# A three-layer graph network on one core: early loads into idle buffers, gamma and beta applied in SBUF, E turned in the freed PSUM bank, new orders on every engine

## The reference, cut to what matters

```python
h = jnp.maximum(_layernorm(x, axis=-1), 0.0)
x_ = h
for l in range(3):
    scores = si[:, :, None] + sj[:, None, :] + attn_b[l]   # si, sj = x_ @ attn_w[l, :d], x_ @ attn_w[l, d:]
    scores = jnp.where(scores >= 0, scores, 0.2 * scores)
    attn = jax.nn.softmax(jnp.where(mask, scores, -jnp.inf), axis=-1)
    h = layernorm(x_ + attn @ x_, g1[l], beta1[l])
    ff = gelu(h @ W1[l] + b1[l]) @ W2[l] + b2[l]            # 256 -> 1024 -> 256
    x_ = layernorm(h + ff, g2[l], beta2[l])
out = x + x_
```

## Time and profile before

| | us |
|---|---|
| median of 3 runs | 1242.56 (1242.36 to 1243.44) |
| the profiled execution | 1241.6 |
| its span | 1239.8 |
| busy: PE, DVE, ACT, POOL | 1196.4, 1075.9, 920.0, 677.4 |

### The profile page before, as it was taken

One profiled execution on the slowest core, in us unless ns is written; L12 is line 12 of the kernel. 1 busy time (PEld: TensorE's weight loads), 2 busy tenths in 40 slices (PEclk: granted clock), 3 DMA queues, 4 the chain that ended last, 5 costly groups with the idle time before them and its releaser, 6 DMA issues.

```text
span 1239.8 us, 23072 instructions
## 1 busy us (share of the span) xinstructions
PE 1196.4 (97%) x7509; PEld 1082.8 (87%) x7509; DVE 1075.9 (87%) x3568; ACT 920.0 (74%) x1754; POOL 677.4 (55%) x648
## 2 busy tenths in 40 slices
PE   2699999999999999999999999999999999999997
PEld 1589999998999999999999999999999999999996
DVE  5899889999998888899998888899989988888865
ACT  3786887678877776778778767777887777677752
POOL 1354455456755554456666545554666455545564
PEclk9999999999999999999999999999999999999999
DMA  7122322233332111222432122122432321122221
GB/s 256 38 77 73 99 70 60 77 94 112 103 103 88 50 44 52 85 71 85 129 114 92 43 59 70 44 69 78 125 115 80 100 60 43 44 69 61 78 89 48
DMA packets 109620, 100.57 MB, mean 81 GB/s; under 512 B 12952, under 2 KB 95932, under 8 KB 109500
## 3 DMA queue, kind: packets, MB, share of 16 engines
q1 hardware_dynamic: 109500, 99.10, 26.3%
HBM read 66.47 MB, written 32.60 MB: 80 GB/s over the span
## 4 chain that ended last, share of the span: by engine, by line
PE 95%; DVE 3%; SPq 1%; DMA 1%; issue 0%; POOL 0%; ACT 0%; DVEq 0%; POOLq 0%
PE acc L1073 44%; PE hbank L1058 42%; PE mix L1087 7%; PE mix L1112 2%; DMA adji<-in_adj_dram 1%; DVE xs L757 0%; DVE junk L694 0%; DVE st L603 0%; DVE st L764 0%; SPq L313 0%; PE util L1104 0%; SPq L332 0%; DVE sc L729 0%; POOL rstd L467 0%; DVE hid_lo L615 0%
## 5 line engine op out<-in xcount | busy, mean ns | idle before, releaser
L1073 PE MATMUL acc<-w2hi,hid_hi 128*128 128x256 f32 x1536 | 442.2, 288 | 0.0
L1073 PE MATMUL acc<-w2hi,hid_lo 128*128 128x256 f32 x1536 | 434.5, 283 | 0.0
L1073 PE MATMUL acc<-w2lo,hid_hi 128*128 128x256 f32 x1536 | 434.4, 283 | 0.0
L912 ACT ACTIVATE hbank<-hbank,vec 128x512 f32<-128x512 f32 x384 | 255.4, 665 | 178.1 <-PE hbank L1058 167.0
L1058 PE MATMUL hbank<-ht_hi,w1hi 128*128 128x512 f32 x768 | 305.7, 398 | 3.6 <-DVE hid_lo L615 2.0
L1058 PE MATMUL hbank<-ht_lo,w1hi 128*128 128x512 f32 x768 | 300.7, 392 | 0.0
L1073 PEld LDWEIGHTS acc<-w2lo,hid_hi 128*128 128x128 f32 x1536 | 294.0, 191 | 6.9
L1073 PEld LDWEIGHTS acc<-w2hi,hid_hi 128*128 128x128 f32 x1536 | 293.9, 191 | 6.9
L1058 PE MATMUL hbank<-ht_hi,w1lo 128*128 128x512 f32 x768 | 299.3, 390 | 0.0
L615 DVE TENSOR_TENSOR hid_lo<-hbank,hid_hi 128x512 fp32r<-128x512 f32 x384 | 259.9, 677 | 39.4 <-ACT hid_hi L918 39.4
L1073 PEld LDWEIGHTS acc<-w2hi,hid_lo 128*128 128x128 f32 x1536 | 293.9, 191 | 0.0
(11 more groups left out here) (80 smaller groups left out, 1708.4 us busy)
## 6 DMA issues: line engine op xcount, KB each, us to landing
z_dram<-tz SPq DMA_DIRECT2D x46, 512.0 KB, 2.6
zt<-z_dram SPq DMA_DIRECT2D x184, 128.0 KB, 2.8
sj_bc<-sj_dram SPq DMA_DIRECT2D x47, 256.0 KB, 3.9
xraw<-in_x_dram SPq DMA_DIRECT2D x16, 512.0 KB, 4.1
out_dram<-xout SPq DMA_DIRECT2D x32, 256.0 KB, 3.0
xres<-in_x_dram SPq DMA_DIRECT2D x15, 512.0 KB, 5.0
xout<-in_L_gnn_W_dram SPq DMA_DIRECT2D x10, 512.0 KB, 5.5
adji<-in_adj_dram SPq DMA_DIRECT2D x16, 256.0 KB, 3.5
```

The lines of the kernel that those rows point to most:

```text
L912: act.activation(hbank[k % HB][:], hbank[k % HB][:], ACT.Gelu, bias=b1c(i.l, c)).then_inc(gelu_n, 1)
L1073: mm = pe.matmul(to, v[:, k % HID, of_g], w[:, i.l, c], start=c == 0 and n == 0 and g % HG == 0, stop=c == C - 1 and n == 2, skip_group_ch ...
```

## The change: what it does, and the diff

- Item 2's x is loaded early into zt; the adjacencies of items 1 and 2 go into the two halves of tz (EARLY = 2). The head's loads are issued in another order.
- From item 2 on ACT applies gamma and beta on the turned rows in place in zt; the cast and the subtraction then read zt, and write ht_hi and ht_lo in blocks. The move of the next z waits for `h_low` in place of `h_out`.
- E is turned in the bank util, which this frees, in place of mix[0]. PE waits before each write of util for all of its readers.
- All lists have another order, the heads' and the slots'. An "o" is item s-2.

```diff
--- before.py
+++ after.py
@@ -43,7 +43,7 @@
 HID = 4
 HB = 3
 PENS = 4
-EARLY = 1
+EARLY = 2
 LEAD = 3
 BY_PE = 2
 QD = 32
@@ -115,7 +115,9 @@
         diag = sb("diag", [P, P], BF16)
         attn_bias = sb("attn_bias", [P, L])
         vec = sb("vec", [P, NV])
-        fence = sb("fence", [P, 1])
+        spare = sb("spare", [P, 1 + L])
+        fence = spare[:, 0:1]
+        attn_part = spare[:, 1:1 + L]
         dots = sb("dots", [P, 3, GG])
         negm = sb("negm", [P, GG])
         den = sb("den", [P, GG])
@@ -131,7 +133,8 @@
 
         vec_rows = sc[0:NV, 0, 0:P]
         b2_rows = hb[:, 1, 0:L]
-        early = [hb[:, i] for i in range(EARLY)]
+        early = [hb[:, 0], zt[:].rearrange("p m a g t -> p (m a g t)").rearrange("p (g d) -> p g d", g=GG)]
+        early_adj = tz[:].bitcast(I32).rearrange("p c g t -> p (c g t)").rearrange("p (i g j) -> p i g j", i=EARLY, g=GG)
 
         def b1c(l, c): return vec[:, l * C + c:l * C + c + 1]
         def dcol(n, l, m):
@@ -158,6 +161,7 @@
         w_in = [sem(f"w_in{i}") for i in range(4)]
         adj_in = sem("adj_in")
         early_in = [sem(f"early_in{i}") for i in range(EARLY)]
+        early_adj_in = [sem(f"early_adj_in{i}") for i in range(EARLY)]
         xraw_in = sem("xraw_in")
         xres_in = sem("xres_in")
         out_sent = [sem(f"out_sent{i}") for i in range(2)]
@@ -232,6 +236,14 @@
                 return early[i.q - 1], early_in[i.q - 1], 16
             return xraw, xraw_in, 16 * (i.g + 1 if i.q == 0 else i.g + 1 - EARLY)
 
+        def by_block(t):
+            return t.rearrange("p (g a t) -> p a g t", g=GG, a=NQ)
+
+        def adj_of(i):
+            if 1 <= i.q <= EARLY:
+                return early_adj[:, i.q - 1], early_adj_in[i.q - 1], 16
+            return adji[:], adj_in, 16 * (i.g + 1 if i.q == 0 else i.g + 1 - EARLY)
+
         def si_of(i):
             return dots[:, 2 * (i.q % 2)]
 
@@ -320,8 +332,10 @@
                 sp.dma_start(t[:], group(x, i.g)).then_inc(arrived, 16)
 
             def load_adj(i):
-                wait(sp, edge_n, i.g)
-                sp.dma_start(adji[:], group(adj, i.g)).then_inc(adj_in, 16)
+                t, arrived, _ = adj_of(i)
+                if arrived is adj_in:
+                    wait(sp, edge_n, 1 if i.q == 1 + EARLY else i.g)
+                sp.dma_start(t, group(adj, i.g)).then_inc(arrived, 16)
 
             def load_weights(n):
                 if n >= len(halves):
@@ -357,7 +371,9 @@
                 if i.q < BY_PE:
                     return
                 sp.wait_ge(z_sent, 16 * moved(i.q))
-                sp.wait_ge(ht_n, KD * i.q)
+                if i.q == BY_PE:
+                    sp.wait_ge(x0_n, GG * (i.q + 1))
+                sp.wait_ge(htlo_n, KD * i.q)
                 for b in range(NQ):
                     sp.dma_start(zt[b * QD:(b + 1) * QD].rearrange("p m a g t -> p m a (g t)"),
                                  z_dram.rearrange("(a p) (m b f) -> b p m a f", a=NQ, b=NQ, m=KD)[b]).then_inc(zt_in, 16)
...
@@ -479,8 +493,8 @@
                 gs = slice(h * HG, (h + 1) * HG)
                 if i.q == 0 and h == 0:
                     pool.wait_ge(ln1_ready, 1)
-                if i.q < EARLY and h == 0:
-                    pool.wait_ge(x0_n, GG * (i.q + 2))
+                if i.q == 0 and h == 0:
+                    pool.wait_ge(x0_n, GG * 2)
                 pool.wait_ge(z1_n, GG * (i.q + 1) if h else GG * i.q + HG)
                 if i.q >= 2:
                     pool.wait_ge(y2_n, 2 * (i.q - 2) + h + 1)
...
@@ -709,8 +727,9 @@
 
                 if i.q == 0:
                     dve.wait_ge(const_set, 5)
-                dve.wait_ge(adj_in, 16 * (i.g + 1))
-                dve.scalar_tensor_tensor(out=pen[:, i.g % PENS], in0=adji[:], scalar=2 * BIG,
+                edges, arrived, count = adj_of(i)
+                dve.wait_ge(arrived, count)
+                dve.scalar_tensor_tensor(out=pen[:, i.g % PENS], in0=edges, scalar=2 * BIG,
                                          in1=diag[:].unsqueeze(1).to_broadcast([P, GG, P]),
                                          op0=ALU.mult, op1=ALU.add).then_inc(edge_n, 1)
                 dve.wait_ge(edge_n, i.g + 1)
...
@@ -773,127 +792,131 @@
 
             def h_low(i, m):
                 dve.wait_ge(hthi_n, KD * i.q + m + 1)
-                dve.tensor_tensor(ht_lo[:, i.q % 2, m], util[:], ht_hi[:, i.q % 2, m].bitcast(F32),
-                                  ALU.subtract).then_inc(htlo_n, 1)
+                if i.q < BY_PE:
+                    dve.tensor_tensor(ht_lo[:, i.q % 2, m], util[:], ht_hi[:, i.q % 2, m].bitcast(F32),
+                                      ALU.subtract).then_inc(htlo_n, 1)
+                else:
+                    dve.tensor_tensor(by_block(ht_lo[:, i.q % 2, m]), zt[:, m],
...
@@ -930,15 +953,17 @@
                                    scale=g1c(i.l, m)).then_inc(ht_n, 1)
                 else:
                     act.wait_ge(zt_in, MOVES_Z * moved(i.q))
-                    act.wait_ge(htlo_n, KD * i.q + m)
-                    act.activation(util[:].rearrange("p (g a t) -> p a g t", g=GG, a=NQ), zt[:, m], ACT.Identity,
+                    act.activation(zt[:, m], zt[:, m], ACT.Identity,
                                    bias=beta1c(i.l, m), scale=g1c(i.l, m)).then_inc(ht_n, 1)
 
             def h_high(i, m):
                 h_out(i, m)
                 act.wait_ge(ht_n, KD * i.q + m + 1)
                 wait(act, ffn1_n, C * (i.q - 1))
-                act.copy(ht_hi[:, i.q % 2, m], util[:]).then_inc(hthi_n, 1)
+                if i.q < BY_PE:
+                    act.copy(ht_hi[:, i.q % 2, m], util[:]).then_inc(hthi_n, 1)
+                else:
+                    act.copy(by_block(ht_hi[:, i.q % 2, m]), zt[:, m]).then_inc(hthi_n, 1)
 
             def leaky(i):
                 act.wait_ge(mask_n, i.q + 1)
@@ -956,9 +981,9 @@
                                    accum_out=den[:, g:g + 1]).then_inc(exp_n, 1)
 
             def et_out(i):
+                wait(act, agg_n, 2 * i.q)
                 act.wait_ge(et_n, i.q + 1)
-                wait(act, agg_n, 2 * i.q)
-                act.copy(ET[:], mix[0][:].rearrange("p g (e i) -> p (g e) i", i=P)).then_inc(eto_n, 1)
+                act.copy(ET[:], util[:].rearrange("p (g i) -> p g i", g=GG)).then_inc(eto_n, 1)
 
             def first_x(i):
                 act.wait_ge(nmr0_n, i.g + 1)
...
@@ -382,26 +398,26 @@
                 sp.dma_start(xraw[:], group(x, NG - 1)).then_inc(last_in, 16)
 
             def slot(s):
-                t, a, d, q6 = item(s - 1), item(s + 2), item(s + 3), item(s + 6)
+                o, t, b, a, d, p, q6 = item(s - 2), item(s - 1), item(s + 1), item(s + 2), item(s + 3), item(s + 4), item(s + 6)
+                if b:
+                    move_z(b)
+                if q6 and q6.l == 0:
+                    load_adj(q6)
+                load_weights(s + 5)
                 if d:
                     send_sj(d)
                 if t and t.l == L - 1:
                     load_xres(t)
+                if p and p.l == 0:
+                    load_xraw(p)
+                if o and o.l == L - 1:
+                    send_out(o, 1)
                 if d:
                     load_sj(d)
-                load_weights(s + 6)
                 if a:
                     send_z(a)
-                if q6 and q6.l == 0:
-                    load_adj(q6)
-                if a:
-                    move_z(a)
                 if t and t.l == L - 1:
                     send_out(t, 0)
-                if q6 and q6.l == 0:
-                    load_xraw(q6)
-                if t and t.l == L - 1:
-                    send_out(t, 1)
                 if s == ITEMS - 4:
                     load_last_input()
 
...
@@ -1088,37 +1112,46 @@
                                    start=g % HG == 0, stop=True, skip_group_check=True)
                 mm.then_inc(agg_n, 1)
 
+            read = {"e": 0, "z": 0, "s": 0}
+
+            def wait_util_read():
+                wait(pe, eto_n, read["e"])
+                wait(pe, htlo_n, read["z"])
+                wait(pe, mask_n, read["s"])
+
             def sj_rows(i):
                 pe.wait_ge(dotj_n, i.q + 1)
                 pe.wait_ge(vec_ready, 1)
+                wait_util_read()
+                read["s"] += 1
                 for g in range(GG):
                     mm = pe.transpose(util[:, g * P:(g + 1) * P], dots[:, 1, g:g + 1].to_broadcast([P, P]), ident[:])
                 mm.then_inc(sj_n, 1)
 
             def z1_turn(i, m):
-                wait(pe, htlo_n, KD * i.q + m)
-                if i.q == 0 and m == 0:
-                    pe.wait_ge(mask_n, 1)
+                wait_util_read()
+                read["z"] += 1
                 for g in range(GG):
                     pe.wait_ge(z1_n, GG * i.q + g + 1)
                     mm = pe.transpose(util[:, g * P:(g + 1) * P], x_of(i)[:, g, m * P:(m + 1) * P], ident[:])
                 mm.then_inc(zt_n, 1)
 
```

(17 more changed lines are left out.)

240 lines of the change are left out of this document (121 added, 119 removed).

## The result

The changed kernel takes 1285.51 us (median of 4 runs, 1281.32 to 1286.02) beside 1242.46 (1241.97 to 1243.44) for the one before, run with it: ratio 1.0338, 95% interval 1.0326 to 1.0351. The forecast was 1238.4, in a range of 1233.0 to 1243.5; it was wrong in sign. None of the rivals was the cause either.

What follows compares the result with a forecast made beforehand. PE was taken as the bound, busy 1196.4 of 1239.8 us. Head -4.3, late ET slots -2.2 and ffn1 cuts +2.3 gave -4.2: 1237.4 profiled, 1238.4 as a median, range 1233 to 1243.5.

Steps and rivals of the forecast that it cites:

- Part 1, the head: First 60 us: earlier loads and new orders let slot 1 begin earlier, taken at -4.3 us, between 0 and 6.5.
- The lower clock: Head: PE may come back at half speed after standing still some 4 us before 48; 0 to 2 us, taken as 0.
- The 1.00: Granted clock shown by the profile windows, set against item 0's slow aggregation (3.78 us, 1.73 later) being a low clock.
- slot 1 begins 4.3 us earlier: End of the head: slot 1 was to begin near 74.5 us in place of 78.85.
- Part 2, E in util: Slots: turning E in util keeps transposes and copy size, and its three new waits are on work long done; 0 us.
- Part 3, in place: Gamma and beta in zt: 0 to 0.1 us for ACT's pair; DVE's low part 0.6 us as before.
- Part 4, the slot of a steady item: ET in time by 0.1 us, late slots gone (-2.2), six ffn1 blocks (+2.3), period near 24.7 us.
- Part 4, SP and DVE in the slots with a new group: DVE's list adds up to 24.9 us, a mask waiting for sj takes 0.6 more, and both hide.
- each us past 1.37: Slots: ffn2 needs the residuals 1.37 us into the slot; without cover, lateness costs PE only the time beyond that.
- (b): Rival, slots: ET is a little late in each, 0.08 us over 45 slots, +3.6, 1242.0 us; chance 0.14.
- (c): Rival, head: it gives little, through lower clock (2 us) and slips in DVE's list (1 or so); 1241.4 us, chance 0.12.
- (d): Rival, slots: z reaches zt late, so its read-out delays ET's copy; 0.26 a slot, 11.7 us, 1250; chance 0.10.

Runs made afterwards that it cites:

- e5_in_place_alone: The kernel before, with its own orders and loads, plus gamma and beta in place in zt and E turned in util: 1257.14 us, ratio 1.0119.
- experiments 1 and 6: 1: sj's load issued earlier in the changed kernel (1284.15, 1285.27 us); 6: work moved to another place in e9_first_no_place (1253.07, 1271.24, 1304.8 us).
- e1_slot: The changed kernel, with SP issuing sj's load right behind sj's own store in every slot: 1284.15 us, ratio 1.034.
- e12_spread: e9_first_no_place with load, moments and shift of a new group at their slots of the kernel before: 1304.8 us, ratio 1.0494.
- e2_both: e1_slot, and in the head item 3's sj load also goes ahead of the late row loads: 1285.27 us, ratio 1.0344.
- experiment 2: The run e8_store_first, which changes SP's order of transfers in the slots: 1258.40 us, ratio 1.0131.
- e15_pen_early: e9_first_no_place with a new group's adjacency load and penalty one slot earlier: 1253.07 us, ratio 1.0086.
- e9_first_no_place: e8_store_first with the in-place part undone (gamma and beta through util again, E turned in mix[0]): 1261.55 us, ratio 1.0152.
- e8_store_first: e2_both, but in the slots SP issues the output's second-half store and xres ahead of sj both ways, then xraw: 1258.40 us, ratio 1.0131.
- e16_pool_old: e9_first_no_place with POOL's h_beta at its place in the kernel before: 1271.24 us, ratio 1.0233.

## Why the prediction was wrong, point by point

- **Part 1, the head.** Right as far as the placing went: item 0's turn of E 20.07 and aggregation 22.29, norm and turn 34.69 (33.6 forecast), the first turn of item 1 at 49.19 (48.05). The lower clock, 0 to 2 and taken at 0, took about 1.5: behind a stop of 2.94 us matmuls of 256 columns come 0.12 apart and then 0.21, and the granted clock of after falls to 0.50:

```profile
50.95 0.38 PE L1097 MATMUL acc<-w2hi,hid_hi 128*128 128x256 f32 x1
51.14 0.42 PE L1097 MATMUL acc<-w2lo,hid_hi 128*128 128x256 f32 x1
...
51.00:54.40 3.40, 3.40 (x13) 2.92 (x13) 3.36 (x17) 2.06 (x6) 2.48 (x3) 0.50 0.00 0
```

  The 1.00 that the prediction set against a low clock in the head was a reading of 10 to 20 us, ahead of the slow aggregation at 27.30, and the trace of before has no granted clock up to 43.7 us. `e5_in_place_alone`, whose head has the same orders, reads 0.50 from 35 to 44 us, where item 1's aggregation is as slow as item 0's.

  What failed was the step "slot 1 begins 4.3 us earlier". It began 1.7 earlier: 1.1 went in DVE's list and 1.5 in the clock. In slot 1 PE then stood 3.39 us for item 3's sj, sent at 70.4, whose way back is issued behind three late row loads (1.3 MB) and takes 6.76 us. That list had been placed up to 52 us and not beyond.
- **Part 2, E in util.** 0, and right: behind the head no wait of PE before util shows.
- **Part 3, in place.** ACT right (0.04, inside the bounds of 0 and 0.1). DVE wrong: "nearest row the split of twice the size, so 0.6 as now". The split of that row ran with POOL idle. Against POOL's multiplications the same form took 1.35, and cost 14.6 us in the old orders. In the new ones it cost nothing more (0.68 to 0.69), which was luck and not the argument.
- **Part 4, the slot of a steady item.** Right: 24.70 forecast as "near 24.7", 24.70 measured; ET in time there, with aggregations of 1.73, six blocks of ffn1 at +0.05.
- **Part 4, SP and DVE in the slots with a new group.** This is the step that failed: "a mask waiting for sj behind x and xres would take 0.6 more ... Both hide; what they cost without that cover is each us past 1.37". Three things were wrong in it. The wait was 3.26 and more: 1.3 MB ahead of sj, of which the store was not counted. What the residual waits for was read for DVE and PE alone; it also needs a store to have ended. And DVE's 24.9 us were summed from undisturbed rows of steady slots; with moments, shift, penalty and what POOL holds up it is 27 to 28, which bounds the slot by itself. The rule ("each us past 1.37") counted only the standing still: behind most stops the granted clock fell to 0.50, another 1.7 us each time, a cost that the prediction had for the head alone. The sizes were wrong throughout: 0.6 stood for waits that made these slots up to 5.4 us too long.
- **Rivals.** (b) and (c) did not come: ET was in time. (d) had the right sign with a chance of 0.10 and the wrong transfer: ACT waited for zt nowhere in the steady slots, and 3.0 us in all between 75 and 1260. z's lateness showed in experiments 1 and 6 (15.3 us in `e1_slot`, 10.4 in `e12_spread`) and in slot 2 of `e2_both`. No rival had a price for DVE as the bound, although the page gave DVE 87% and the prediction itself had DVE's list end 0.3 us into the next slot.

What of the 43 us has a run behind it: 27 go with SP's order (experiment 2), and 8.5 with a penalty in the same slot as moments and shift (`e15_pen_early` against `e9_first_no_place`, which itself stands 3.2 above `e8_store_first`). What is left, 10.6, is 9.6 in the spans of the profiled executions (1249.4 and 1239.8). By its periods 2.6 lie in slot 2, 8.0 in the clusters, 6.2 of them in their first slots, where penalty and moments still meet, and 2.2 in the +0.05 of all 44 slots; the 2.2 of the late slots before and some 1.1 us of the head go against them, which makes 9.5. Whether another order of POOL's list would win the clusters' 8.0 back stays open: `e16_pool_old` shows that it matters, by 10 us in the wrong direction, and no better one was tried.

## What to carry to other kernels

Add an engine's list up in the slot that has most to do, not in a steady one, and take DVE's durations from rows where POOL runs beside them: the same instruction had 0.29 and 1.4 us here. In front of a transfer that an engine waits for in order, count every byte that its queue issues first, stores too, and read all that the buffer behind it waits for. When one wait in the head is taken away, ask what the next load in the same queue is before the gain is counted: 6.0 us became 2.4.

## What the runs showed of the hardware

- DVE's smallest instructions are held as long as its large ones: a scalar_tensor_tensor on 4 elements a partition took 0.16 us alone and 1.13 beside POOL, and the mask 0.38 or 1.4. A tensor_scalar with one SBUF operand (`norm2`) is held as well: 400 ns alone, 658 in the long slots; in the mean of the first two layers 653 in after against 428 before, in the last layer 554 against 429. Beside POOL's power of 128x4 (1.07 us) a low part with two SBUF operands was not held (0.69, `e5_in_place_alone`); the port rule cited above, as it is worded, would have it wait.
- A load of 256 KB from DRAM to all partitions took 7.51 us from issue to landing behind 1.3 MB, and a 256 KB store 8.1 behind sj's transfers and two loads of 512 KB (in `e1_slot`).
- Stopping for 3 us can cost PE more than the 3 us: its next 36 matmuls took 6.0 in place of 4.31, at a granted clock of 0.50 for 3.4 us of them. Yet in the head, where DVE set the next wait, keeping its clock up won nothing.
